# One-hots made tile by tile with a partition scalar, and adjacency slices without gaps

## What is computed

```python
def rgcn_conv(x, src, dst, etype, W, root, bias):
    n = x.shape[0]
    seg = dst * R + etype
    x_src = x[src]
    agg = jax.ops.segment_sum(x_src, seg, num_segments=n * R)
    cnt = jax.ops.segment_sum(jnp.ones((src.shape[0],), x.dtype), seg, num_segments=n * R)
    agg = jnp.where(cnt[:, None] > 0, agg / jnp.maximum(cnt, 1.0)[:, None], 0.0)
    agg = agg.reshape(n, R, -1)
    return jnp.einsum('nrd,rdk->nk', agg, W) + x @ root + bias
```

## Time and profile before

| | |
|---|---|
| time, median of 3 runs | 7473.25 us (7442.04 to 7475.92) |
| time of the profiled execution | 7472.03 us |
| its span | 7469.8 us, 91271 instructions |
| granted clock of TensorE, mean | 0.793 |
| TensorE busy | 5533.5 us (74%), 35088 matmuls |
| VectorE busy | 2387.7 us (32%) |
| ScalarE busy | 2078.3 us (28%) |
| GpSimd busy | 3856.8 us (52%) |
| DMA packets | 689816, 903.43 MB |

### The profile page before, as it was taken

The page is one execution under the profiler, slowest core; times in us unless marked ns, Lnnn a source line. Parts: engine busy times, 40 slices in busy tenths (PEclk is TensorE's granted clock), DMA queues, the critical chain, the costliest instruction groups (busy, mean ns, idle before and its releaser), DMA issues.

```text
span 7469.8 us, 91271 instructions
## 1 busy us (share of the span) xinstructions
PE 5533.5 (74%) x35088; PEld 3186.3 (43%) x35088; DVE 2387.7 (32%) x5451; ACT 2078.3 (28%) x3054; POOL 3856.8 (52%) x3575
## 2 busy tenths in 40 slices
PE   2777799956677666777667546888888878888887
PEld 1454466523333333333333233444444544454444
DVE  6776641233333333433333211111111211111112
ACT  2444430046565655666555000000000000000000
POOL 4000000076666666767665553666666656666665
PEclk6888899956666666666666566999999989999999
DMA  2222226433333333333333223455455444444443
GB/s 72 118 85 101 97 103 239 185 98 109 91 103 95 109 87 98 102 101 98 101 95 101 67 83 110 140 168 167 137 169 163 140 150 142 145 143 137 138 143 108
DMA packets 689816, 903.43 MB, mean 121 GB/s; under 512 B 73166, under 2 KB 605444, under 8 KB 685412
## 3 DMA queue, kind: packets, MB, share of 16 engines
q1 hardware_dynamic: 335292, 453.57, 18.0%
q0 software_dynamic: 169216, 348.44, 16.8%
q10 hardware_dynamic: 184872, 95.53, 4.4%
HBM read 692.22 MB, written 205.05 MB: 120 GB/s over the span
## 4 chain that ended last, share of the span: by engine, by line
PE 44%; ACT 12%; issue 9%; another core or an unknown queue 8%; DVE 4%; ACTq 2%; DVEq 0%; DMA 0%; POOL 0%; POOLq 0%
PE bank L1421 21%; ACT stage L1523 12%; PE bank L1386 7%; PE bank L1461 4%; PE bank L1462 4%; PE bank L1401 3%; PE bank L1444 2%; ACTq L1532 2%; PE bank L1390 1%; DVE scaled L1690 1%; PE bank L1463 1%; PE bank L1464 1%; DVE type_scaled L1690 1%; PE bank L1470 1%
## 5 line engine op out<-in xcount | busy, mean ns | idle before, releaser
L1373 POOL DMA_INDIRECT messages<-table,src_rows x2552 | 2873.0, 1126 | 1582.2 <-issue 711.9
L1421 PE MATMUL bank<-slices,pieces 128*128 128x384 fp8e4 x10290 | 1983.5, 337 | 363.8 <-issue 351.1
L1523 ACT CAST stage<-bank 128x490 fp8e4<-128x490 f32 x1344 | 1458.5, 1270 | 1063.8 <-PE bank L1401 820.0
L1421 PEld LDWEIGHTS bank<-slices,pieces 128*128 128x128 bf16 x10290 | 988.5, 100 | 1206.1 <-issue 702.3
L1373 POOL DMA_INDIRECT messages<-table,rel_rows x940 | 900.0, 957 | 586.1 <-issue 251.4
L1401 PE MATMUL bank<-rel_hot,lo_dense_hot 128*128 128x490 bf16 x1344 | 647.2, 521 | 675.3 <-ACT stage L1523 506.7
L1386 PE MATMUL bank<-group_hot,messages 128*128 128x120 bf16 x10476 | 875.6, 245 | 238.4 <-issue 99.8
L1651 DVE TENSOR_TENSOR sums<-sums,bank 128x120 f32 x873 | 236.5, 271 | 2299.9 <-remote 1823.0
L1386 PEld LDWEIGHTS bank<-group_hot,messages 128*128 128x128 bf16 x10476 | 777.0, 113 | 395.5 <-issue 239.3
L1650 DVE TENSOR_TENSOR type_sums<-type_sums,bank 3x120 f32 x403 | 107.9, 268 | 1913.2 <-PE bank L1390 1280.6
L1355 POOL IOTA iota_rel_i<- 128x490 int32 x1 | 1.4, 1395 | 1355.8 <-DMA table<-typed_rows 1355.8
(11 more groups left out here) (249 smaller groups left out, 4344.6 us busy)
## 6 DMA issues: line engine op xcount, KB each, us to landing
slices<-relations_d SPq DMA_DIRECT2D x140, 768.0 KB
adjacency_d<-adjacency SPq DMA_DIRECT2D x15, 4704.0 KB, 14.5
adjacency<-adjacency_d SPq DMA_DIRECT2D x15, 4704.0 KB, 15.0
slices<-relations_d SPq DMA_DIRECT2D x70, 816.0 KB
relations_d<-stage ACTq DMA_DIRECT2D x168, 320.0 KB
messages<-table,src_rows POOLq DMA_INDIRECT x2552
inverse<-inverse_d SPq DMA_DIRECT2D x52, 640.0 KB
relations_d<-stage ACTq DMA_DIRECT2D x84, 340.0 KB
```

The lines of the kernel that those rows point to most:

```text
L1373: pool.indirect_dma_start(messages[:, i % MESSAGES, t, 0:ROWS[v]], None, GATHERED[v], bass.IndirectOffsetOnAxis(ap=rows[:, e:e + 1], axis= ...
L1421: mm = pe.matmul(bank[DENSE_BANKS[K % 2]][:, 0:CHUNK], pieces[M % PIECE_RING][:, tile % PIECE_TILES, piece * P:(piece + 1) * P], slices[:, ...
L1523: act.copy(stage[:, u % 2, :, 2 * m:2 * m + 2], bank[REL_BANKS[p % 2]][:, 0:REL_COLS].rearrange("p (c d) -> p c d", d=2), saturate=False). ...
```

## The change

Three edits that belong together.

1. The codes stay one float of 32 bits for each edge. The copy to pairs of half floats (L615) goes; `code_f` itself is spilled to `code_d` and loaded as `group_code`. Both transfers have the same bytes as before, 4 for each edge.
2. The one-hot of a group is made by four operations instead of one, one for each tile of 128 edges: the iota of 120 columns is compared with a scalar that each partition has for itself (the code of its edge). The last of the four signals. The wait in front of them is the same.
3. The slice buffer is laid out flat, so that a slice of 16 tiles has no gaps: its DMA writes one run of 6144 bytes in each partition instead of 12 of 512, and the moving operand of a dense matmul steps by 512 bytes from stage to stage in such a slice, and by 544 in one of 17 tiles, as before. The number, order and waits of the transfers are the same, and so is the size of the ring.

```diff
@@ prep_vector
-                step(vec.tensor_copy(code2[:, :, :], code_f.unsqueeze(2).broadcast_to([P, EDGE_TILES, 2])))
                 vec.sem_inc(codes_made, 1)
@@ prep_sync
-            sp.dma_start(code_d, code2[:, :, :].rearrange("p t n -> p (t n)")).then_inc(spilled, 16)
+            sp.dma_start(code_d, code_f).then_inc(spilled, 16)
@@ SyncE in the SAGE block
-                    sp.dma_start(group_code[:, :, :].rearrange("p t n -> p (t n)"), code_d).then_inc(rgcn_in, 16)
+                    sp.dma_start(group_code[:, :], code_d).then_inc(rgcn_in, 16)
@@ the buffers
-        (slices,), slices_end = lay(types_end, ("slices", [P, SLICE_RING, CHUNK_STAGES, SLICE_TILES[0] * STAGE_NODES], f8))
+        (slices,), slices_end = lay(types_end, ("slices", [P, SLICE_RING, SLICE_TILES[0] * CHUNK], f8))
@@ conv_sync, load_slice
-                to = slices[:, J % SLICE_RING, :, 0:SLICE_TILES[n] * STAGE_NODES].bitcast(bf16)
-                sp.dma_start(to, relations_d[c, :, r, cols].rearrange("p (s h) -> p s h", s=CHUNK_STAGES)).then_inc(slice_in[J % 2], 16)
+                sp.dma_start(slices[:, J % SLICE_RING, 0:SLICE_TILES[n] * CHUNK].bitcast(bf16), relations_d[c, :, r, cols]).then_inc(slice_in[J % 2], 16)
@@ conv_tensor, dense
+                slice_of_chunk = slices[:, J % SLICE_RING, 0:SLICE_TILES[n] * CHUNK].rearrange("p (s h) -> p s h", s=CHUNK_STAGES)
                 mm = pe.matmul(bank[DENSE_BANKS[K % 2]][:, 0:CHUNK], pieces[M % PIECE_RING][:, tile % PIECE_TILES, piece * P:(piece + 1) * P],
-                               slices[:, J % SLICE_RING, :, within * STAGE_NODES:(within + 1) * STAGE_NODES], start=(at == 0), stop=(at == TASK_STEPS - 1))
+                               slice_of_chunk[:, :, within * STAGE_NODES:(within + 1) * STAGE_NODES], start=(at == 0), stop=(at == TASK_STEPS - 1))
@@ conv_vector, onehots
-                shape = [P, GROUP, GROUP_COLS // 2, 2]
-                vec.tensor_tensor(group_hot[:, i % MESSAGES, :, :].rearrange("p k (c t) -> p k c t", t=2),
-                                  iota16[:, 0:GROUP_COLS].rearrange("p (c t) -> p c t", t=2).unsqueeze(1).broadcast_to(shape),
-                                  group_code[:, g * GROUP:(g + 1) * GROUP, :].unsqueeze(2).broadcast_to(shape), ALU.is_equal).then_inc(group_hot_made, 1)
+                for t in range(GROUP):
+
+                    op = vec.tensor_scalar(group_hot[:, i % MESSAGES, t, :], iota16[:, 0:GROUP_COLS], group_code[:, g * GROUP + t:g * GROUP + t + 1], None, ALU.is_equal)
+                op.then_inc(group_hot_made, 1)
```

More of the change, by code:

```diff
@@ L183, in resnorm_gnn @@
     row_rel_d = dram("row_rel_d", (P, EDGE_TILES), i32)
-    code_d = dram("code_d", (P, 2 * EDGE_TILES), f16)
+    code_d = dram("code_d", (P, EDGE_TILES))
     invdeg_d = dram("invdeg_d", (1, NODES_PADDED))
@@ L276, in resnorm_gnn @@
         (x_f,), _ = lay(X_ROWS, ("x_f", [P, NODE_TILES, P], f32))
-        (dst_T, typ_T, row_src, row_rel, code2, limit, base_f), tiles_end = lay(
+        (dst_T, typ_T, row_src, row_rel, limit, base_f), tiles_end = lay(
             A1, ("dst_T", [P, TILES_PADDED], f32), ("typ_T", [P, TILES_PADDED], f32), ("row_src", [P, TILES_PADDED], i32),
-            ("row_rel", [P, EDGE_TILES], i32), ("code2", [P, EDGE_TILES, 2], f16),
+            ("row_rel", [P, EDGE_TILES], i32),
             ("limit", [1, GROUPS], f32), ("base_f", [1, GROUPS], f32))
@@ L286, in resnorm_gnn @@
             ("emb_1", [NODE_TYPES, RELATIONS * WIDE], f32), ("emb_root", [NODE_TYPES, WIDE], f32),
-            ("src_rows", [P, EDGE_TILES], i32), ("group_code", [P, EDGE_TILES, 2], f16))
+            ("src_rows", [P, EDGE_TILES], i32), ("group_code", [P, EDGE_TILES], f32))
         (count_of,), count_of_end = lay(weights_end, ("count_of", [P, RELATIONS, NODE_TILES], f32))
```

## The result

The changed kernel takes 7527.01 us in the median of four runs (7520.98 to 7538.7), the kernel before, on the same chip, 7461.24 (7442.04 to 7475.92): a ratio of 1.0082, 95% interval 1.006 to 1.0104. It is slower by 0.8%, some 61 us by ratio. The profiled execution took 7520.98 us, its span is 7519.2, 49.4 longer than that of before.

What follows compares the result with a forecast made beforehand. TensorE's loop with ScalarE plus finishes paces the first convolution; gathers with buffer waits fill the later two, VectorE having slack. From 7472.03 us, -1.9 + 6 + 12 + 0 gives 7488, range 7375 to 7580 (own range 7450 to 7510).

Steps and rivals of the forecast that it cites:

- +6 us: VectorE's finishes: 40 places by up to 0.29 us make 12, half taken; elsewhere the longer chain hides in VectorE's waits.
- rival 1: Later convolutions: four one-hot operations keep GpSimd out like one chain, +68 to 115 us, say 7565; chance 0.20.
- The copy, -1.9 us: Preparation: removing the code copy takes 1.84 us, and 0.02 around it, off VectorE's serial chain to the row addresses.
- The chain, 0.69 us (0.49 to 0.89): One-hots: four operations of 0.24 us, overlapping by 0.09, replace one of 0.40 us, 873 times; 253 us more VectorE.
- the cover: VectorE's waiting, 1.8 us and more, with one-hots made four groups ahead, hides the longer chain; without it +253 us.
- The gathers, +12 us (0 to 115): Later convolutions: chains may reach into gathers, up to 0.29 us (0.49 longest) in each of 235 pairs; a sixth of 68 taken.
- the "against" of the rival: The argument against rival 1: GpSimd may get in between two of the four one-hot operations.
- The fixed part of an operation: One-hots: the skill page gives 92 ns an operation, 0.37 us for four; the forecast kept the profile row's 0.15 us.
- The slices, 0: Slice transfers: gapless ones are a little quicker, but nothing waits for them, so no change in time.
- Rivals 2 and 3: Later convolutions: fewer transfer pieces ease TensorE's pauses, 7370 us, chance 0.17; the 512-byte stride slows dense matmuls, 7790, chance 0.04.
- Rival 4: Later convolutions: one-source operations leave GpSimd alone, gathers shorten, at most -24 us in the third; 7440, chance 0.07.
- What bounds the later convolutions: Eight gathers, then a 1.86 to 2.21 us wait for a buffer: 11.77 us a pair of groups, 2766 of 2885 us.

Runs made afterwards that it cites:

- the second comparison: Against the kernel before (7402 us, slow chip): slices alone 1.0001, four-operation one-hots everywhere with gapped slices 1.0116, those one-hots in the later two convolutions only 1.0003.
- the two kernels with longer and shorter ones: On quick chips: the kernel before with four two-tensor one-hots (longer gathers), 1.0003; the changed kernel with one-hots behind the addition (shorter gathers), 0.9998 and 1.0002.
- the run with another order: The changed kernel with the one-hot of group i+4 behind group i's addition and dense one-hots, against the kernel before on quick chips: 0.9998 and 1.0002.
- The idle comparisons with an immediate scalar: The kernel before plus unread comparisons behind each first-convolution one-hot, on quick chips: three 1.0006 and 1.0002, six 1.0002; three behind the new one-hots 0.9975.

## Why the prediction was right or wrong, point by point

The forecast was 7488 us, the range 7375 to 7580; 7527 is in it, but above my own range of 7450 to 7510, in the part that I gave 0.28 (slower by over 0.5%), not in the 0.53 of no difference. The rise over the kernel before was forecast as 16 us and came as 61. The term that failed is +6 us for VectorE's longer chain, and behind it the reading of what bounds the kernel. That the time still lies in the range is in part luck: its upper end was set by rival 1, gathers held up in the later convolutions, and that is not where the time went; and on a quick chip the same kernel takes 6842 us.

- *The copy, -1.9 us.* The operation is gone, but the steps ahead of it came later (the addition at L613 starts at 88.12 us, before 86.26), so the maximum that follows the copy starts at 91.96 instead of 91.99. The first gather is 0.6 us later. The 1.9 us didn't arrive: the step behind the long wait for a DMA starts 0.95 us later (64.51, before 63.56), two more such waits are 0.2 and 0.5 us longer, and one short operation (L611) takes 0.62 instead of 0.36. Whether the change makes them longer or one execution differs from the next by that is open.
- *The chain, 0.69 us (0.49 to 0.89).* Measured 717.9 / 873 = 0.82. One operation has a median of 247 ns, as taken (0.24), and starts 0.16 after the last, so an undisturbed chain is 3 x 0.16 + 0.25 = 0.73. The rest is mostly hold-up by GpSimd, which I had not thought of: below. VectorE came to 2748.2 us, inside 2467 to 2816.
- *What hides it, +6 us (0 to 12).* The first convolution lost 37.7 us in the profiled pair, and 58 to 62 in the second comparison. The bound of 12 was too low. I had counted the places where a wait for VectorE stands in the profile, times the added length. The loss is not in these waits alone (they grew by 42.5 us in one pair, by 0.5 in the other). It appears only where waits end late with no release that the profile can trace, the "remote" of the earlier trace rows, which the sum left out. With the cover gone altogether the text had put 253 for all stages; 403 groups of 0.42 would be 169 in the first, and 22 to 36% of that came. Whether the length of the chain is the cause on the slow chips is not shown: all kernels that would tell length from kind and place ran on quick chips, where length costs nothing.
- *The gathers, +12 us (0 to 115), rival 1.* Wrong in its mechanism: the chain doesn't act as one. Gathers of the second and third convolution take 964 and 971 ns after, before 957 and 971; with the new one-hots in these stages alone the ratio is 1.0003. A single new operation does hold a gather. In these stages 82 gathers began when one had run for over 0.05 us and had over 0.14 us to go: 68 ended 0.82 us behind its end, the longest took 1.02 us, and all together lost 3 us. The operations of the chain that follow don't hold it further, which is the "against" of the rival. The sentence of the Trainium skill ("SBUF — State Buffer", on the DVE blocking DMA), that GpSimd can't write descriptors while VectorE works in a mode with two ports, agrees with the trace for the new operations, with 0.08 us at most for a gather; that sentence doesn't speak of operations with two tensors, and those hold a gather here too (1.16 us). In the first convolution I had put the chain behind the dense ones at 97 us more for GpSimd; its gathers took 75 us less (1885 instead of 1960), as GpSimd gets in when the dense one ends, though the new chain has begun. Four operations with two tensors in the same place held 268 gathers to the end of the fourth, so there the kind of the operation matters; why is open.
- *The fixed part of an operation.* The sentence on the Trainium skill ("VectorE: DVE Perf Modes", TRN2 errata) would have had the four at 0.37 us together, no longer than one; the row was right, it is twice that. The same section says below its table that the row of 58 cycles under-predicts a single operation and that about 150 were measured; by that one would be an estimated 0.19 us and four 0.75. Here one takes 0.25 and the four, which overlap, 0.73.
- *The slices, 0.* Right: 1.0001, packets down by 197 000, dense matmuls at 336 ns. Rivals 2 and 3 fall with it.
- *Rival 4* (chance 0.07: the change gives back what it disturbs) has its first half right: the gathers are shorter, though in the first convolution and not in the later ones where I had sought it. On the slow chips GpSimd is freed in the same way (1216 to 1169 ns in the first convolution) and only waits longer (for TensorE 629.6 us, before 541.4). On quick chips the kernel gains 0.25%, but not by the shorter gathers, as the two kernels with longer and shorter ones show. What brings the gain is open.
- *What bounds the later convolutions.* The wait of 1.9 to 2.2 us behind eight gathers and TensorE's pauses don't belong to the kernel: none of the nine traces from quick chips, the changed kernel's among them, has a "remote" wait in the second convolution. Taking them for the kernel's own rhythm was sound for this chip and wrong as a general statement.
- One correction to the section on the kernel: in the loop the one-hot of group i + 4 stands ahead of the addition of group i, not behind it. Where a finish or dense one-hots lie between two additions, these come before the one-hot, and the run with another order shows that the place matters (0.27%).

## What to carry to other kernels

Splitting one operation into four for the sake of a cheaper operand form costs three fixed parts, here 0.16 us each: the chain takes 0.82 us where the one operation took 0.40. For GpSimd beside them it was then the length of the single operation that counted, not that of the chain. A sum over the waits that the profile of before names is not a bound, when the same profile has hundreds of microseconds in waits that it can't name. And a result near 1% should be measured on more than one chip and at more than one time before it is believed: here its sign is not the same in all comparisons.

## What the runs showed of the hardware

- *The kernel before differs by 8 to 9% between chips (or hours), and not by the clock.* It took 7461 and 7402 us in two comparisons, 6854 to 6861 in four; the granted clock was 0.79 to 0.81 in all traces. On the slow chips work behind TensorE's signal for a group comes late: in the changed kernel the addition of 5133.67 us had waited 7.83 us for a release that the profile can't trace, and GpSimd's wait ended within 0.13 us of it. Count the time from the end of a group's last recorded matmul to its addition. In the first 338 of the 403 groups of the first convolution it was over 2 us in 27 to 31 groups with the old one-hots (154 to 183 us together) and in 42 and 45 with the new ones (225 and 219), in all five traces from slow chips; in the nine from quick chips it was so in 20, with either. In the 470 groups of the later convolutions it was so in 252 to 282 on slow chips, with either, and in 0 to 7 on quick ones. Since the ends of matmuls are modelled, this can be a late signal or a matmul that ends later than recorded. What makes it late, and why it is so more often with the new one-hots, is open.
- *A partition-scalar operation is held by a gather, at one point.* Its duration goes by when it begins relative to a running gather: 0.24 to 0.25 us for starts up to 0.45 us into it, 0.42 for a start at 0.50 to 0.55, then falling back (0.34 at 0.6, 0.26 at 0.7). So an operation that begins in this stretch ends 0.96 to 1.00 us into the gather. The idle comparisons with an immediate scalar show the same (0.40 us for starts at 0.50 to 0.55 and 0.33 at 0.6 in the median, 0.16 to 0.17 outside). The chain of 0.90 at 5133.86 is such a case, its last operation starting 0.54 us into the gather of 5133.80. The row of all 3492 shows the spread (ns, shortest, median and longest):

```profile
L1628 DVE TENSOR_SCALAR group_hot<-iota,group_code x3492: 219/247/502, 1488.6 to 7479.5; 128x120 bf16<-128x120 f16 x194
```

The two-tensor operation of before stayed at 0.40 us wherever it began inside a gather, and so did the four short ones at 0.21. They hold GpSimd up and are not held; the one with a partition scalar does both.
- *Four two-tensor operations are shorter than four with a partition scalar*: 209 against 274 ns in the mean for the same 120 columns, with starts 0.13 and 0.16 us apart.
